# A new order of the twelve units of a step in the scan phase of a Mamba-style block, and of the side jobs between them

## The reference

```python
def step(h, inp):
    ul, dl, Bl, Cl = inp
    dA = jnp.exp(dl[..., None] * A)
    h = dA * h + (dl * ul)[..., None] * Bl[:, :, None, :]
    y = jnp.einsum('bkdn,bkn->bkd', h, Cl)
    return (h, y)
...
x_dbl = jnp.einsum('bkdl,kcd->bkcl', xs, x_proj_w)      # ranks, B and C
dts = jnp.einsum('bkrl,kdr->bkdl', dts, dt_proj_w)
delta = jax.nn.softplus(dts + dt_proj_b[None, :, :, None])
out_y = _selective_scan(xs, delta, A, Bs, Cs, Dk)
```

## Time and profile before

| quantity | value |
|---|---|
| time, median of 3 runs | 12441.71 us (12428.21 to 12448.03) |
| the profiled execution: its time, its span | 12428.21 us, 12426.3 us |
| busy, whole span: PE, DVE, POOL, ACT | 10745.4, 10724.7, 9752.4, 8061.8 us |
| granted TensorE clock, mean | 0.851 of 2.4 GHz |
| longest groups: GpSimd L913, VectorE L739 with carry from PSUM | 7213.5 us (3072 times), 4479.2 us (1920 times) |

### The profile page before, as it was taken

One profiled execution on the slowest core, in us unless ns is written; L12 is line 12 of the kernel. 1 busy time (PEld: TensorE's weight loads), 2 busy tenths in 40 slices (PEclk: granted clock), 3 DMA queues, 4 the chain that ended last, 5 costly groups with the idle time before them and its releaser, 6 DMA issues. The chain is left out here.

```text
span 12426.3 us, 236253 instructions
## 1 busy us (share of the span) xinstructions
PE 10745.4 (86%) x91896; PEld 5926.8 (48%) x91896; DVE 10724.7 (86%) x6806; ACT 8061.8 (65%) x13314; POOL 9752.4 (78%) x4238
## 2 busy tenths in 40 slices
PE   8978888888888888888888888888888887799999
PEld 5644444444444444444444444444444443678778
DVE  7789999999999999999999999999999998555554
ACT  3366777677777776777677767776777775444443
POOL 2178999899999999999999989998999998433330
PEclk9977888788878887888788878887888887799999
DMA  3344554455445554555455545544554454221220
GB/s 107 110 111 113 123 133 114 111 123 133 115 112 129 133 116 112 128 132 116 112 129 132 118 109 128 132 113 114 124 130 113 115 123 116 68 62 47 62 62 11
DMA packets 380191, 1363.70 MB, mean 110 GB/s; under 512 B 55270, under 2 KB 55974, under 8 KB 375756
## 3 DMA queue, kind: packets, MB, share of 16 engines
q1 hardware_dynamic: 379084, 1348.57, 46.0%
HBM read 983.45 MB, written 364.90 MB: 109 GB/s over the span
## 5 line engine op out<-in xcount | busy, mean ns | idle before, releaser
L913 POOL TENSOR_TENSOR HC<-H,crep 128x1024 f32<-128x1024 f32 x3072 | 7213.5, 2371 | 836.0 <-DVE H L739 831.4
L739 DVE TENSOR_TENSOR_SCAN H<-E,car,psum 128x1024 f32<-128x1024 f32 x1920 | 4479.2, 2343 | 232.0 <-PE psum L639 174.1
L823 ACT ACTIVATE E<-dlr,am 128x1024 f32<-128x1024 f32 x2560 | 2917.0, 1142 | 68.0 <-DVE H L739 65.6
L597 PE MATMUL psum<-sx,selb 96*128 96x512 f32 x4864 | 2192.0, 560 | 694.9 <-DVE H L739 419.9
L661 PE MATMUL psum<-HC,sely 128*32 128x512 f32 x12288 | 2519.3, 706 | 5.9 <-POOL HC L913 5.1
L639 PE MATMUL psum<-diag,dluT 128*32 128x128 f32 x49152 | 1933.2, 317 | 681.4 <-DVE H L739 676.0
L717 DVE TENSOR_TENSOR psum<-dur,psum 128x1024 f32<-128x1024 f32 x1792 | 2167.9, 1210 | 179.4 <-PE psum L597 175.2
L639 PEld LDWEIGHTS psum<-diag,dluT 128*32 128x32 f32 x49152 | 1624.4, 128 | 1307.2 <-DVE H L739 1176.5
L597 PEld LDWEIGHTS psum<-sx,selb 96*128 96x128 f32 x4864 | 1016.5, 242 | 2141.1 <-DVE H L739 862.5
L739 DVE TENSOR_TENSOR_SCAN H<-E,psum 128x1024 f32<-128x1024 f32 x640 | 1455.1, 2283 | 89.6 <-PE psum L639 68.7
L807 ACT ACTIVATE diag<-idn,blt 128x128 f32<-128x128 f32 x4096 | 1335.4, 394 | 4.1
(11 more groups left out here) (135 smaller groups left out, 11216.4 us busy)
## 6 DMA issues: line engine op xcount, KB each, us to landing
dur<-scr_dlu SPq DMA_DIRECT2D x1024, 384.0 KB, 6.8
dlr<-scr_dl SPq DMA_DIRECT2D x1024, 384.0 KB, 6.8
scr_dl<-dlt SPq DMA_DIRECT2D x256, 384.0 KB, 3.0
scr_dlu<-dlu SPq DMA_DIRECT2D x256, 384.0 KB, 6.8
scr_yk<-yt SPq DMA_DIRECT2D x256, 384.0 KB, 8.3
yp<-scr_yk SPq DMA_DIRECT2D x128, 384.0 KB, 8.8
scr_xa<-xs SPq DMA_DIRECT2D x64, 384.0 KB, 3.5
scr_sz<-xs SPq DMA_DIRECT2D x64, 384.0 KB, 3.4
```

Source lines behind the costliest of these rows:

```text
L597: r = e.matmul(o[:, sub * 512:(sub + 1) * 512], selb[:, which, :], sx[:, c % 2, sub * 512:(sub + 1) * 512], start=True, stop=True)
L739: e.tensor_tensor_scan(H[:, un % NH, ::step], decay[:, ::step], drive[:, ::step], init, ALU.mult, ALU.add).then_inc(scan_done)
L823: e.activation(o, dlr[:, slot(m, j), :], ACT.Exp, scale=am[:, ae:ae + 1]).then_inc(exp_done)
L913: e.tensor_tensor(HC[:, un % NHC, :], H[:, un % NH, :], crep[:, g, :], ALU.mult).then_inc(hc_done)
```

## The change

The two rows of `ORDER` are replaced. Each chunk keeps 14 direct, 6 diagonal and 4 pooled units, at other positions: now nearly every diagonal or pooled unit has a direct one on both sides, and three direct units in a row are left at even x 0 to 2 and odd x 6 to 8. `project` moves from even x 9 and 10 to 5 and 7, and `split` from even x 11 to 8. The `delta` of the next even step moves from odd x 1 to even x 9, that of the next odd step from odd x 9 to 3. `turn_dlu`, `turn_b`, the `rep` and the diagonals move as well, `held` follows them, and SP's transfers are put in another order. The durations of single instructions and their numbers are left as they are.

```diff
@@ -312,11 +312,10 @@
     NBLK = TC // 128
     GPOOL, GDIAG = 1, 3
     DIRECT, POOLED, DIAGONAL = 0, 1, 2
-    ORDER = ((1, 0, 0, 0, 2, 3, 2, 3, 1, 3, 1, 2), (1, 3, 1, 3, 1, 3, 0, 0, 0, 2, 2, 2))
+    ORDER = ((0, 0, 0, 1, 1, 1, 2, 3, 2, 3, 2, 3), (0, 3, 0, 3, 0, 3, 2, 2, 2, 1, 1, 1))
     KIND = tuple(tuple(DIAGONAL if g == GDIAG else POOLED if g == GPOOL and x in pooled else DIRECT for x, g in enumerate(row))
-                 for row, pooled in zip(ORDER, ((8, 10), (2, 4))))
-    REPS = (None, 1, 0, 3, 2)
-    DIAG_EVEN, DIAG_ODD = {0: 3, 1: 4, 2: 4, 3: 4}, {6: 3, 7: 3, 8: 3, 9: 3, 10: 2, 11: 3}
+                 for row, pooled in zip(ORDER, ((3, 5), (9, 11))))
+    REPS = (0, None, 3, 1, 2)
     wx = T("wx", [C, NK, 2, C + NR])
     dtw = T("dtw", [C + NR, NK * ND])
     dtb = T("dtb", [C, NK * 2])
@@ -471,10 +470,10 @@
     for n in range(NSTEP):
         c = n // 2 + 1
         if n % 2 == 0:
-            order += [("rep", c - 1, i) for i in range(3, 5) if n] + [("lt", n + 1)]
-            order += [("x", c)] if c < NCHUNK else []
+            order += [("rep", c - 1, i) for i in range(2, 5) if n] + [("lt", n + 1)]
+            order += [("x", c), ("dt", n + 2)] if c < NCHUNK else []
         elif c < NCHUNK:
-            order += [("dt", n + 1), ("bt", c), ("rep", c, 0), ("lt", n + 1), ("dt", n + 2), ("rep", c, 1), ("rep", c, 2)]
+            order += [("bt", c), ("dt", n + 2), ("lt", n + 1), ("rep", c, 0), ("rep", c, 1)]
     for job, last in zip(order[1:], order):
         if last[0] == "rep":
             held[job] = (rep_out, rep_index(*last[1:]) + 1)
@@ -547,25 +546,27 @@
         for n in range(NSTEP):
             if n % 2 == 0:
                 if n:
-                    in_dlr(n + 1)
-                    out_dlu(n + 1)
-                if ends_image(n + 1) and n + 2 < NSTEP:
-                    load_u(n // 32 + 1)
-                if n:
-                    in_dur(n + 1)
+                    if not ends_image(n + 1):
+                        out_dlu(n + 1)
+                        in_dur(n + 1)
                     store_y(n - 1)
                 load_y(n + 1)
             else:
                 if n + 1 < NSTEP:
                     out_dl(n + 1)
+                    out_dlu(n + 1)
+                    in_dur(n + 1)
                     in_dlr(n + 1)
                 store_y(n - 1)
-                if n + 1 < NSTEP:
-                    out_dlu(n + 1)
-                    in_dur(n + 1)
                 load_y(n + 1)
                 if n + 2 < NSTEP:
                     out_dl(n + 2)
+                    if ends_image(n + 2):
+                        out_dlu(n + 2)
+                        if n + 3 < NSTEP:
+                            load_u(n // 32 + 1)
+                        in_dur(n + 2)
+                    in_dlr(n + 2)
         store_y(NSTEP - 1)
         e.wait_ge(y_stored, 16 * NSTEP)
 
@@ -684,26 +685,23 @@
             if n == NSTEP:
                 continue
             if n % 2 == 0:
-                if x < 2 and n:
-                    rep(c - 1, x + 3)
-                if x == 7:
-                    turn_dlu(n + 1, 0)
-                    turn_dlu(n + 1, 1)
-                if x in (9, 10) and c < NCHUNK:
-                    project(c, x - 9)
+                if x < 3 and n:
+                    rep(c - 1, x + 2)
+                if x in (3, 4):
+                    turn_dlu(n + 1, x - 3)
+                if x in (5, 7) and c < NCHUNK:
+                    project(c, (x - 5) // 2)
+                if x == 9 and c < NCHUNK:
+                    delta(n + 2)
             elif c < NCHUNK:
                 if x == 1:
-                    delta(n + 1)
-                if x == 5:
                     turn_b(c)
-                if x == 6:
-                    rep(c, 0)
-                if x in (7, 8):
-                    turn_dlu(n + 1, x - 7)
-                if x == 9:
+                if x == 3:
                     delta(n + 2)
-                if x in (10, 11):
-                    rep(c, x - 9)
+                if x in (6, 7):
+                    turn_dlu(n + 1, x - 6)
+                if x in (8, 10):
+                    rep(c, (x - 8) // 2)
 
     def vector(e):
         def split(c):
@@ -752,7 +750,7 @@
             if kind(un) == DIRECT:
                 multiply(un)
             scan(un)
-            if c < NCHUNK and n % 2 == 0 and x == 11:
+            if c < NCHUNK and n % 2 == 0 and x == 8:
                 split(c)
 
     def scalar(e):
@@ -849,7 +847,7 @@
             rep(0, i)
         e.wait_ge(a_made, 2)
         exp(0)
-        diagonal(0, 0, sum(DIAG_ODD.values()))
+        diagonal(0, 0, 18)
         for un in range(NUNIT + 12):
             n, x = divmod(un, 12)
             c = n // 2 + 1
@@ -861,29 +859,27 @@
             if n == NSTEP:
                 continue
             if n % 2 == 0:
-                if x < 3 and n:
-                    rep(c - 1, x + 2)
-                if x in DIAG_EVEN:
-                    diagonal(c - 1, sum(DIAG_ODD.values()) + sum(DIAG_EVEN[i] for i in range(x)), DIAG_EVEN[x])
-                if x == 8:
+                if 1 <= x <= 3 and n:
+                    rep(c - 1, x + 1)
+                if x < 7:
+                    diagonal(c - 1, 18 + 2 * x, 2)
+                if x == 5:
                     turn_dlu(n + 1)
-                if x == 11 and c < NCHUNK:
+                if x == 8 and c < NCHUNK:
                     project(c)
+                if x == 10 and c < NCHUNK:
+                    delta(n + 2)
             elif c < NCHUNK:
                 if x == 2:
-                    delta(n + 1)
-                if x == 6:
                     turn_b(c)
+                if x == 5:
+                    delta(n + 2)
                 if x == 7:
-                    rep(c, 0)
-                if x == 8:
                     turn_dlu(n + 1)
-                if x == 10:
-                    delta(n + 2)
-                if x == 11:
-                    rep(c, 1)
-                if x in DIAG_ODD:
-                    diagonal(c, sum(DIAG_ODD[i] for i in range(6, x)), DIAG_ODD[x])
+                if x in (9, 11):
+                    rep(c, (x - 9) // 2)
+                if x >= 6:
+                    diagonal(c, 3 * (x - 6), 3)
 
     def pool(e):
         def delta(m):
@@ -922,16 +918,14 @@
             if n == NSTEP:
                 break
             if n % 2 == 0:
-                if x in (4, 5):
-                    multiply(12 * n + 2 * x)
-                if x == 11:
-                    multiply(12 * (n + 1) + 2)
+                if x in (0, 2):
+                    multiply(12 * n + 3 + x)
             else:
-                if x == 1:
-                    multiply(12 * n + 4)
-                if x == 4 and n + 1 < NSTEP:
+                if x == 0 and n + 1 < NSTEP:
                     delta(n + 1)
-                if x == 11 and n + 2 < NSTEP:
+                if x in (3, 5):
+                    multiply(12 * n + 6 + x)
+                if x == 8 and n + 2 < NSTEP:
                     delta(n + 2)
 
     run_block(nc, sync, tensor, vector, scalar, pool)
```

## The result

The changed kernel takes 12631.28 us in the median of 4 runs (12624.23 to 12653.4), beside 12444.87 us (12428.21 to 12449.38) for the one before on the same chip: 1.0155 times as long, 95% interval 1.0138 to 1.0173. The profiled execution took 12636.41 us, 208 more than that of before, or 1.63 us in each of 128 chunks. The forecast was +130 us, 12570.

What follows compares the result with a forecast made beforehand. VectorE was taken as the bound, idle 4.45 us a chunk; new idle 4.5 + 1.0 = 5.5, so 1.0 more times 128 = 130 us on 12428 gives 12558, the median 13 above: 12570 us, range 12470 to 12680.

Steps and rivals of the forecast that it cites:

- VectorE's 72.3 us stay, its idle time moves: Scan phase: instruction numbers and lengths stay, so VectorE's busy 72.3 us a chunk stay; only the 4.45 us idle changes.
- Diagonals behind direct units lose their waits: Six diagonal fills a chunk get 3.45 us of cover from a direct unit; about 2 us of waits go.
- A half of `project` in front of the diagonal of even x 7 is the largest term: `project` at even x 5 and 7 delays unit 7's diagonal fill and `split`; about 4.5 us of idle time a chunk.
- The full-clock walk: Even x 5 to `split` at full clock: x 7 waits 0.7, 1.6 or 2.6 us; mean sum 2.55 us.
- The low-clock walk: Same place starting at low clock: sums 3.5 us (even k), 5.3 (k = 1), 7.5 (k = 3), mean 4.95.
- `delta` at odd x 3 and the other diagonals, 1.0 us: Odd x 1, 3, 5 and even x 11: occasional low-clock waits, 1.0 us a chunk, between 0 and 2.2.
- GpSimd, ScalarE, SP and the load of u cost nothing: Other engines and transfers keep enough slack or lead; no new waits, 0 us.
- GpSimd among the releasers of L737: A sign against the prediction: GpSimd showing up as what releases VectorE's waits at source line L737.
- Full clock at the projection: Rival: clock stays full at even x 5, idle time 3.05 us a chunk, 12260 us; chance 0.24.
- The low clock that persists through both halves: Rival: low clock through `project` and the next fill, idle time about 8 us, 12860 us; chance 0.10.
- The chunks: Sign in chunk lengths: k = 3 longest, near 80 us; k = 0 and 2 near 76.
- The clock at even x 4 and 5: Sign: TensorE's clock there should be 0.5 to 0.7; a full clock would prove the prediction wrong.

Runs made afterwards that it cites:

- e9: The changed kernel with `project` at even x 8 and 10, `split` at odd x 0, the two `delta` at odd x 1 and 5: 12441.26 us, ratio 0.9997.
- e3: The changed kernel with the fills of six direct units (even x 0, 1, 2, 4, odd x 8, 10) issued three times: 12661.98 us, ratio 1.0153.
- e5: The changed kernel with `turn_dlu` alone moved from even x 3 and 4 to behind `delta` at even x 10: 12595.54 us, ratio 1.0121.
- e12: e11 without the repeated fills: 12739.88 us, ratio 1.0226.
- e4: The changed kernel with `project` at even x 3 and 4, `split` at x 6 and both halves of `turn_dlu` at x 10: 12534.14 us, ratio 1.0052.
- e1: The kernel before with only the new unit order and what must follow it; `project`, `delta`, `turn_dlu` at their old places: 13026.75 us, ratio 1.0445.
- e11: e9 with fills of even x 1, 2 and odd x 10 issued twice, and `delta` moved from odd x 5 to 8, `rep` behind it: 12778.43 us, ratio 1.0261.
- e6: The kernel before with fills of odd x 1, even x 2 to 4 and odd x 10 and 11 repeated: 12475.37 us, ratio 1.0026.
- e7: The kernel before with only the diagonal fill of odd x 1 issued twice: 12405.3 us, ratio 0.9965.

## Why the prediction was right, step by step

- **VectorE's 72.3 us stay, its idle time moves.** Right: 9247.77 us busy beside 9259.8, and 1.63 us more per chunk.
- **Diagonals behind direct units lose their waits.** Right. The diagonal at odd x 3 had 1.46 us and has under 0.1; the one at even x 9 had 0.47 and has under 0.1. That is 1.9 us against the 2 put down.
- **A half of `project` in front of the diagonal of even x 7 is the largest term.** Right in place and mechanism, shown by the timeline after and by e9, where `project` stands elsewhere and 190 us come back.
- **The full-clock walk.** Right to about 0.1 us where its conditions held: 0.8, 1.72 and 2.51 us in e3 for the walk's 0.7, 1.6 and 2.6. Its means at full clock, 1.65, 1.95, 1.74 and 2.94, lie above that for two reasons: the last chunk of a direction projects the next one, which the walk did not see and which hardly changes its mean over the four directions, and some chunks wait longer at the same clock, for which the repeated spreads in front are a likely cause, not a shown one.
- **The low-clock walk was mis-sized.** I took low clock in 8 chunks of 10 and 4.3 us until it is back. It was half at the end of the scan of x 4 in 119 chunks of 127, and for another 6.5, 4.8, 6.2 and 5.9 us for k = 0 to 3. So the sum ran its full 1.9 us, not 1.3, and the half of `project` held up the next job 2.4 us, not 1.7. x 7 waits 4.5, 3.6, 4.4 and 5.1 us in such chunks, where I had 3.3, 4.0, 3.3 and 5.2. The section from x 7 to `split` cost 5.5 us (4.34 + 0.30 + 0.9) instead of 4.5.
- **`delta` at odd x 3 and the other diagonals, 1.0 us.** Too much: odd x 3 and 5 and even x 11 come to 0.5. With the 4.4 us of waits before, 5.5 + 0.5 - 4.4 = 1.6 us, where I had 5.5 - 4.45 = 1.0. Two errors of opposite sign left the forecast 61 us short of the measured median, so that it came as near as it did is in part luck.
- **GpSimd, ScalarE, SP and the load of u cost nothing.** Nearly: waits for HC are 21.2 us in 6 pieces, 0.2% of the time. I had said that GpSimd among the releasers of L737 would prove me wrong; as a sign that was too strict, since these 21 us decide nothing.
- **The rivals.** Full clock at the projection: it wasn't, and e3 shows what it would have been worth there, 1.5 to 3 us in a chunk. The Trainium skill, "TensorE: Matmul & The Clock Gate", section "Why this matters for your kernels", advises to avoid long gaps between bursts. The order after has no pause like the 3.19 us of the earlier trace rows in front of these fills. In the whole scan phase TensorE has 4 pauses over 3 us where it had 68, and the mean clock is 0.853 beside 0.851. The low clock that persists through both halves: no, it came back during the wait. Its sum had a slip: 8 us less 4.45 is 3.55, not 3.3, so 454 us and not 420.
- **The chunks.** k = 3 is the longest, as said, 80.1 us in the mean of all; k = 0 and 2 take 78.8 and 78.5 and not 76, which is the same mis-sized term. The clock at even x 4 and 5 was 0.52, within the 0.5 to 0.7 that I had put down.

Why k = 1 gained: it has no extra matmul in front of the sum, so its wait at x 7 is the smallest, and before it had the largest idle time, with a slow half of `project` in front of `split` and a wait of 1.6 us at odd x 11. Where it projects its own direction, its halves are slow as before.

What stays open: what sets how long the clock stays at half in a given stretch. e5 and e12 show that it changes when work in front is moved, in a direction that I could not foretell, and e4 that busy work does not always lift it. e1's new waits for the exp of ScalarE (149.6 us) are read from one trace and not tried by a run of their own.

## What to carry to other kernels

When jobs move on an in-order engine, add up what stands between a buffer's release and the wanted fill, at both clock levels, and set it against the consumer's time; the totals of busy time say nothing of it. Give the unit with the long fill no side job in front: that one place decided this change. And treat work moved from one place as added at another until its new place is walked too (e4, e11).

## What was not expected of the hardware

- Work of TensorE without a pause does not bring the clock back soon: in the stretches above it is busy for all 11.3 us from 6963.4 to 6974.7 at 0.50. In the earlier trace rows it was 16.85 of 17.00 us.
- Four matmuls of `project` over u read across rows (every 64th element) take 3.59 to 3.74 us in the changed kernel, the same at a clock of 0.50 (3.74) as at 1.00 (3.59 in most). Read in a row they take 1.88 us at 1.00 and 2.7 where the clock is 0.7 in the mean. So in a slow read the clock makes next to no difference, and in e4 the half clock outlasts two of them in a row. The Trainium skill, "SBUF — State Buffer", section "Door 1: The DMA port swizzle (why `[64,N]` ≈ `[32,N]`)", has a note on 16-byte lines, by which fp32 may be read for free up to a stride of four elements. The factor of two here agrees with its direction; no run varied the stride.
- Repeating fills whose result is the same raised the mean clock from 0.85 to 0.91 (e3) and 0.90 (e6), and the kernels became no faster. A single repeat in an idle place gave 0.35% (e7).
